# A GCN and Mamba stack on one core: stage A takes its tiles from last to first, multiplies adj by known x1 columns there, and the rest is one stream over the scans

## The reference, cut to what matters

```python
def gnn(x1, x2):                              # L = 3, W: 128 x 128
    ax1, ax2 = 2 * (adj @ x1), 2 * (adj @ x2)      # eps is 0: ax + (1 + eps) * ax
    for i in range(3):
        ax1 = relu(ax1 @ W1[i].T + b1[i]); ax2 = relu(ax2 @ W2[i].T + b2[i])
    return concatenate((ax1, ax2), 1) @ Wm.T + bm
x1 = layernorm(x + gnn(x, x2))
h = layernorm(relu(adj @ x1 @ gcn_w + gcn_b)) * ln_g + ln_b
xz = h @ w_in; u = silu(causal_conv4(xz[:, :256])); z = xz[:, 256:]
dt, B, C = split(u @ w_xp); dt = softplus(dt @ w_dt + b_dt)
for t in range(4096):                         # 256 channels x 16 states
    state = exp(dt[t] * A) * state + dt[t] * B[t] * u[t]
    y[t] = state @ C[t]
out = layernorm(x1 + ((y + u * D) * silu(z)) @ w_out)
```

## Time and profile before

| | us |
|---|---|
| median of 3 runs (1179.34 to 1181.56) | 1180.63 |
| profiled execution | 1176.16 |
| its span | 1174.6 |
| TensorE busy (with overlapping records) | 1017.3 |
| VectorE busy | 1058.9 |
| ScalarE (ACT) busy | 515.5 |
| GpSimd busy | 325.1 |

### The profile page before, as it was taken

One profiled execution on the slowest core, in us unless ns is written; L12 is line 12 of the kernel. 1 busy time (PEld: TensorE's weight loads), 2 busy tenths in 40 slices (PEclk: granted clock), 3 DMA queues, 4 the chain that ended last, 5 costly groups with the idle time before them and its releaser, 6 DMA issues. The chain is left out here.

```text
span 1174.6 us, 13465 instructions
## 1 busy us (share of the span) xinstructions
PE 1017.3 (87%) x4242; PEld 703.8 (60%) x4242; DVE 1058.9 (90%) x864; ACT 515.5 (44%) x914; POOL 325.1 (28%) x208
## 2 busy tenths in 40 slices
PE   2789999989999999999988989989889798785665
PEld 1567776767777777444555646656556455553454
DVE  5899999999999998713999999999989999999995
ACT  3344333333334242224555555736456456455431
POOL 5100101000000101001245273463632734537330
PEclk9899999999999999999998999989999899795666
DMA  9999999999999999847444253254442532101000
GB/s 259 247 189 326 318 317 330 317 335 303 348 302 350 308 335 271 174 160 257 148 150 165 91 193 139 84 190 149 145 155 80 196 143 73 36 20 53 20 26 9
DMA packets 190907, 226.43 MB, mean 193 GB/s; under 512 B 8608, under 2 KB 164320, under 8 KB 176528
## 3 DMA queue, kind: packets, MB, share of 16 engines
q1 hardware_dynamic: 107008, 165.69, 44.3%
q10 hardware_dynamic: 80768, 52.70, 18.3%
q0 software_dynamic: 3088, 7.54, 2.3%
HBM read 162.72 MB, written 63.18 MB: 192 GB/s over the span
## 5 line engine op out<-in xcount | busy, mean ns | idle before, releaser
L774 DVE STREAM_TRANSPOSE at<-rows 128x1024 f32<-128x1024 f32 x136 | 267.0, 2003 | 27.1 <-DMA rows<-in_adj 14.9
L979 PE MATMUL yT<-ah,xh 128*128 128x512 f32 x512 | 214.1, 418 | 54.5 <-DVE al L782 54.5
L486 POOL TENSOR_TENSOR dBuP<-dtu,b_sb 128x1024 f32<-128x1024 f32 x64 | 166.0, 2594 | 271.0 <-DVE hs L915 208.0
L527 ACT ACTIVATE ah<-at 128x2048 fp32r<-128x2048 f32 x64 | 122.5, 1913 | 241.0 <-PE yT L979 229.9
L1066 PE MATMUL bank<-adjc,xm 128*128 128x512 f32 x448 | 216.8, 614 | 0.8 <-ACT axT L591 0.8
L979 PE MATMUL yT<-al,xh 128*128 128x512 f32 x512 | 201.4, 393 | 0.0
L979 PE MATMUL yT<-ah,xl 128*128 128x512 f32 x512 | 201.3, 393 | 0.0
L1148 PE MATMUL yT<-ident,pr 128*128 128x128 f32 x1024 | 160.8, 312 | 24.0 <-DVE pr L922 24.0
L915 DVE TENSOR_TENSOR_SCAN hs<-dA,zero,dBuP 128x1026 f32<-128x1026 f32 x64 | 166.9, 2609 | 8.3 <-ACT dA L681 8.3
L681 ACT ACTIVATE dA<-dt,A_sb 128x512 f32<-128x512 f32 x256 | 169.4, 712 | 9.2 <-POOL dt L467 6.4
L1148 PEld LDWEIGHTS yT<-ident,pr 128*128 128x128 f32 x1024 | 142.3, 163 | 49.7 <-DVE pr L922 33.8
(11 more groups left out here) (148 smaller groups left out, 1049.0 us busy)
## 6 DMA issues: line engine op xcount, KB each, us to landing
adjT<-at SPq DMA_DIRECT2D x56, 1024.0 KB, 7.8
adjc<-adjT SPq DMA_DIRECT2D x56, 1024.0 KB, 4.9
rows<-in_adj SPq DMA_DIRECT2D x152, 256.0 KB, 8.9
rows<-in_adj ACTq DMA_DIRECT2D x136, 256.0 KB, 9.1
b_sb<-b_dram ACTq DMA_DIRECT2D x32, 512.0 KB, 3.8
xm<-in_x SPq DMA_DIRECT2D x4, 512.0 KB, 15.7
xs<-in_L_gnn_x SPq DMA_DIRECT2D x4, 512.0 KB, 14.9
res<-in_x POOLq DMA_DIRECT2D x8, 256.0 KB, 7.6
```

The source lines that it names most:

```text
L486: nc.gpsimd.tensor_tensor(dBu(n, par)[:, :, 1:], dtu[par][:, :, :], b_sb[pair % 2][:, nB(n) % 2:nB(n) % 2 + 1, :].to_broadcast([P, H, TILE ...
L527: nc.scalar.activation(ah[c % 2][:, :], at[c % 2][:, :, :].rearrange("p m t -> p (m t)"), ACT.Copy)\
L774: last = nc.vector.transpose(dst.rearrange("p m (g i) -> p g m i", i=32), src.rearrange("p g (i m) -> p g m i", i=32))
L979: last = mm(acc[k][:, :], w[:, b, :], v[c % 2][:, cols], start=(b == 0 and j == 0), stop=(b == KB - 1 and j == 2))
```

## The change

1. Stage A goes through the tiles from 7 to 0 (`t` is the step, `i = 7 - t` the tile, `s` the place of a chunk in its step). Tile j's x1 is normed in step 8-j and split into fp32r parts `x1h`, `x1l` a step later (`split_x1`). Columns with known x1, `c >= i + 2`, get the third product in stage A: 12 matmuls more in `extra`, which add into `accB`; 21 chunks in all. The partial sums of tiles 1 to 5 go through DRAM (`part_dram`), tile 0's stays in `accB`. These chunks aren't stored.
2. Tile 7's chunks are needed again, since x1 isn't known at first: they are read and transposed a second time and stored, two in each of the steps 4 to 7 (`AGAIN`), at `s` = 2 and 5. 41 chunks are stored, where it was 56.
3. After stage A, tile 0 lacks 8 blocks (chunks 1 and 0, still in `at`), four of them behind the last norm; tile 1 has 12 blocks; the other tiles have 152, where they had 192. `BLOCKS` lists them, `STEPS` and `stream()` share them out over windows 0 to 5 as one sequence, and `front_ax` follows as each sum is done.
4. The norm writes x1 straight into `xm`. The order of its rows is that of a reordering in the third layer's ACT write (and of y's copy later), so `mid`, its loads, and the residual's loads go. ACT issues the output's stores.
5. For tile 0, z is made ahead of the convolution, in banks of its own. The gcn of tile 1 stands ahead of window 0.
6. The tap transposes move into step 1. `adjc` now lies where `rows` was, so its first loads wait for the last transposes of stage A. All loops are written out.

```diff
+ORDER = [tuple(range(CHUNKS))] * (TILES - 1) + [(3, 4, 5, 6, 7, 2, 0, 1)]
+FIRST = TILES - 1
+AGAIN = {(t, s): 2 * (t - 4) + k for t in range(4, TILES) for k, s in enumerate((2, 5))}
+def known(i):
+    return range(i + 2, CHUNKS)
+def sequence():
+    seq = []
+    for t in range(TILES):
+        for s in range(CHUNKS):
+            i, c = TILES - 1 - t, ORDER[t][s]
+            seq.append((i, c, CHUNKS * t + s, t > 0 and i > 0 and c not in known(i)))
+            if (t, s) in AGAIN:
+                seq.append((FIRST, AGAIN[t, s], None, True))
+    return seq
...
+BLOCKS = [(a, j, m) for a in range(1, TILES) for j in ((1, 2, 0) if a == 1 else range(min(a + 2, CHUNKS))) for m in range(CH)]
...
+            def transpose(n):
+                dve.wait_ge(rows_in[n % NROWS], 16 * Q * (n // NROWS + 1))
+                if n >= 2:
+                    k = SEQ[n - 2][2]
+                    if k is not None:
+                        dve.wait_ge(chunk_low, k + 1)
+                    if SEQ[n - 2][3]:
+                        dve.wait_ge(chunk_stored[n % 2], 16 * stored_before(n))
...
+            def stage_a(t):
+                for s in range(CHUNKS):
+                    k = CHUNKS * t + s
+                    transpose(AT_N[k])
...
+                    if k > 0 and (t, s - 1) not in AGAIN:
+                        lo(k - 1)
...
+                    if t > 1 and s == 2:
+                        split_x1(t - 2)
+                    if t > 0 and s == 6:
+                        norm_stats(t - 1)
+                    if t > 0 and s == 7:
+                        norm_apply(t - 1)
+                    if (t, s) in AGAIN:
+                        transpose(AT_N[k] + 1)
+                        lo(k)
...
+            def extra(t, s):
+                i, c = TILES - 1 - t, ORDER[t][s]
+                pe.wait_ge(x1_low, TILES - c)
+                if c == EXTRA_FIRST[t] and t > 2:
+                    pe.wait_ge(part_copied, t - 2)
+                for m in range(CH):
+                    b = CH * (c - JX) + m
+                    cols = slice(m * TILE, (m + 1) * TILE)
+                    for j, (w, v) in enumerate(((x1h, ah), (x1l, ah), (x1h, al))):
+                        last = mm(accB[:, :], w[:, b, :], v[s % 2][:, cols], start=(c == EXTRA_FIRST[t] and m == 0 and j == 0),
+                                  stop=(i > 0 and c == CHUNKS - 1 and m == CH - 1 and j == 2))
+                return last
...
             for l in range(LAYERS):
                 layer(TILES - 1, l)
+                tile0(1, l, l + 1)
             merge(TILES - 1)
+            tile0(1, LAYERS, CH)
+            tile0(0, 0, CH)
...
             front_gcn(0)
+            adj_blocks(range(0, 7))
             front_tr(0)
+            adj_blocks(range(7, 8))
+            front_z(0, 0)
+            front_z(0, 1)
             front_xc(0, 0, TAPS)
             front_xc(0, TAPS, H * TAPS)
             front_dbc(0, 0)
+            adj_blocks(range(8, 9))
             front_dtp(0, 0)
             pe.wait_ge(selectors_ready, 4)
             spread_B(0, 0, 0)
+            adj_blocks(range(9, 12))
+            front_gcn(1)
+            for b in range(TILES):
+                window(b, b % 2, b > 0, b < TILES - 1)
```

More of the change, by code:

```diff
@@ L110, in gnn_mamba @@
         A = ExitStack()
+        NROWS = 4
+        rows = [sb(f"rows{k}", [P, GROUPS, P], F32, A) for k in range(NROWS)]
         xh = [sb(f"xh{k}", [P, KB, D], F32R, A) for k in range(2)]
@@ L299, in load_x @@
                         .then_inc(x_in[2 * part + k], 16)
-            load_rows(sp, (0, 1), 0, 0)
+            load_rows(sp, (0, 1), 0)
             load_x(0)
             for c in range(1, NROWS):
-                load_rows(sp, (0, 1), 0, c)
+                load_rows(sp, (0, 1), c)
                 load_x(c)
[L307 to L314, removed]
@@ L330, in load_adj @@
[L330 to L336, removed]
@@ L338, in load_res @@
[L338 to L353, removed]
@@ L356, in _ @@
[L356 to L364, removed]
+            for n, (i, c, k, st) in enumerate(SEQ):
+                sp.wait_ge(chunk_turned, n + 1)
+                if st:
+                    sp.dma_start(adjT[((i - 1) * CHUNKS + c) * P:((i - 1) * CHUNKS + c + 1) * P, :],
+                                 at[n % 2][:, :, :].rearrange("p m t -> p (m t)")).then_inc(chunk_stored[n % 2], 16)
+                if n + NROWS < len(SEQ):
+                    load_rows(sp, (0, 1), n + NROWS)
@@ new lines, in _, with adj_blocks @@
+            tile0(0, 0, CH)
+            def adj_blocks(ks):
+                for k in ks:
+                    a, j, m = BLOCKS[k]
+                    q = k // CH
+                    begins = k == 0 or BLOCKS[k - 1][0] != a
+                    ends = k + 1 == len(BLOCKS) or BLOCKS[k + 1][0] != a
+                    if begins:
+                        pe.wait_ge(ax1_ready, a)
+                        if a in PARTS:
+                            pe.wait_ge(part_loaded, 16 * a)
+                            mm(accB[:, :], ident[:, :], part_in[:, :], start=True, stop=False).then_inc(part_used, 1)
+                    if m == 0:
+                        pe.wait_ge(adjT_in[q % NADJ], 16 * (q // NADJ + 1))
+                    last = mm(accB[:, :], xm[:, CH * j + m, :], adjc[q % NADJ][:, m, :], start=(begins and a not in PARTS), stop=ends)
+                    if ends:
```

517 lines of the change are left out of this document (262 added, 255 removed).

## The result

The changed kernel takes 1211.2 us, median of four runs (1206.3 to 1212.5), against 1180.9 beside it: ratio 1.0251, 95% interval 1.0220 to 1.0281. It is slower, as forecast, but by twice as much: 30.3 us where 14.7 were forecast, and 1195.3 us with a range up to 1206. The profiled executions differ by more, 1212.5 against 1176.2 us, spans 1210.7 against 1174.6, because the one of before lay under its median and this one over it.

What follows compares the result with a forecast made beforehand. VectorE bounds stage A and the scan windows, TensorE the handover between. Terms: stage A +49.3, handover -18.3, first window -10.9, windows -5.4, together +14.7 us on the median 1180.6, giving 1195.3 us, range 1177 to 1206 (own course 1188 to 1201).

Steps and rivals of the forecast that it cites:

- The change's sign and its reason: Whole kernel: slower, chance 0.80; blocks taken out of VectorE-bound windows give nothing, anything put into stage A costs time.
- Stage A, TensorE: Stage A: up to step 5 TensorE's 61.6 us a tile fits VectorE's 63.1; then TensorE sets the end, +49.3 us.
- The begin of the heavy stretch: Stage A, `lo` of step 6, place 3: done at 405.3 against 377.6, with store waits +6 and -2.3 us.
- TensorE's last stretch: Stage A from step 6, place 3: eleven heavy chunks, two plain ones and the MLP take 110 us, ending at 515.3.
- rival A: End of stage A: VectorE, not TensorE, ends it; end -9.6 us, 1185.7 us; chance 0.15.
- rival C: Stage A: stores of chunks read again land late, 3.3 us for each of five, +10.5, 1205.8 us; chance 0.11.
- rival B: Stage A: fewer stores relieve traffic, VectorE's chunk 6.0 not 6.30 us, sum -2.5, 1178.1 us; chance 0.14 for it or more.
- Handover: Last product of stage A to first scan: 60.1 us instead of 78.4, -18.3 us.
- the term for the clock: Handover: half clock behind TensorE's uncovered 4.5 us wait costs 2.5 us, bounds 0 and 3.4 (two stretches).
- rival D: Handover: not shortened as far, another chain takes 3 to 5 us of the 18, 1199 us; chance 0.08.
- First window: Scan 0 to scan 1: gcn of tile 1 stands before window 0, scan 1 at 550.3 rather than 561.2, -10.9 us.
- Windows: Scan windows: 40 blocks leaving give nothing; unrolled loops -3.1, small waits for spread banks 2.3 less; -5.4 us.

Runs made afterwards that it cites:

- experiment 4: Changed kernel with early x1 products for tiles 0 and 1 only, blocks of tiles 2 to 5 back in the windows: 1193.7 us, ratio 1.0118.
- experiment 1: Changed kernel with one matmul (x1h ah) instead of three in the early product: 1188.6 us, ratio 1.0076.
- experiment 3: Changed kernel with second readings moved: to places 1 and 3 of steps 4 to 7, 1217.3 us; all eight in steps 6 and 7, 1202.0 us.
- experiment 5: Changed kernel with chunks of three stacks placed between chunks of two in steps 4 to 6: 1207.6 us, ratio 1.0241.
- experiment 2: Changed kernel without second readings, tile 7's chunks stored in step 0: 1204.7 us, ratio 1.0213.
- experiment 6: Changed kernel with nine unread filler products in TensorE's two longest handover waits: 1208.3 us; also with ACT's relu moved later in window 0: 1209.3 us.
- experiment 7: Kernel before the change with the loops over windows 2 to 5 written out on all engines: 1178.9 us, ratio 0.9999.
- experiment 8: Changed kernel, early products for tiles 0 and 1 only, fillers; eight chunks stored in step 0: 1181.1 us; last, two stored, six reread in steps 6, 7: 1175.0.

## Why the prediction was right in direction and wrong in size

**The change's sign and its reason** stood: blocks moved out of windows that VectorE bounds bring nothing and cost in stage A (experiment 4: the edit for 10 chunks, 15.6 us, for nothing), and the handover and the first window give back less than stage A takes.

**The step that failed** is the one in "Stage A, TensorE": "Up to `t` = 5 a tile ... still fits into VectorE's 54.3 + 0.85 + 7.9 = 63.1." The 63.1 us hold only for steps 4 and 5, which have two readings each. Step 3 has none: VectorE's sum is 54.3 + 0.85 = 55.2 us, and TensorE's by the same prices (216 matmuls and the layers) 56.1, so it didn't fit even as a sum. The step took 55.9 us (norms at 172.80 and 228.67), and TensorE didn't wait between 189 and 237 us. For steps 4 and 5 the comparison is right as a sum, and both engines have room in it, but they don't have it at the same time. `ah` and `al` have two buffers, so neither can be more than two chunks ahead. Behind a second reading TensorE has nothing to do (4.35 us at 304.17), and during its 8.15 us chunks VectorE waits for `ah`. Measured: 14.9 us of waiting ahead of step 6, place 3, gone to 0.3 without the ten chunks (experiment 4), and to 3.8 in all with lighter ones (experiment 1). I had put 0 for it. The begin of the heavy stretch came 8.9 us later than predicted; the sum had 3.7 us for stores, and the store waits there are 5.3 us, where the kernel before had 4.5 up to the same chunk, so that term was too high by 2.9 and hid part of the miss. The waits view of before also has 4.2 us of short waits of its transposes for `lo`, which the changed kernel's doesn't have: 14.9 - 2.9 - 4.2 leaves 7.8 of the 8.9. How the waits come about is settled in part. Most of them, 12.2 of 14.9 us, stand at the second chunk of a step, where ACT's `ah` comes behind the end of TensorE's last heavy chunk and behind the copy of the partial sum (324.10). The place of the second readings (experiment 3) isn't it, the clustering (experiment 5) at most a third. The copies, the half clock behind TensorE's waits (1.6 us at 304) and a third `ah` buffer weren't tried apart.

**TensorE's last stretch** was sized right: 110 us, measured 111.3, and 109.8 in experiment 4. So rival A (VectorE ends the stage) was wrong. The row's 0.2265 us a matmul held in the changed kernel. The 215.7 ns of TensorE: Matmul & The Clock Gate, of the Trainium skill ("Wait — 56ns, not 53.3ns?"), would have given 4.8 us less for the stretch and isn't seen.

**Stores** (rival C) were not the reason: 1.2 us a reading predicted, 0.26 to 1.65 shown. They can be: 11.9 us with the readings at places 1 and 3.

**Traffic relief** (rival B) didn't come: a `lo` or transpose takes what it took, and the store waits are 5.3 us where they were 4.5. Storing eight more in step 0 does cost: the first norm came 11.9 us later in experiment 2.

**Handover.** All operations ran as listed; the term for the clock was mis-sized. I took 2.5 us for one to two stretches at half clock of 3.4 us, as the trace of before showed one. It was some 14 us, in two stretches of 7. That is at most 7 us lost, an estimate that takes TensorE for the chain's pace all through. Filling the two waits gave 4.5 us and the predicted 3.7 us for the eight matmuls (experiment 6), with 7 us near half clock left. The 2.4 us behind ACT's relu I hadn't seen at all: of the moved gcn of tile 1 I costed TensorE's side, and not what ACT's relu has queued behind it. In all 5.2 us of the 18.3 were missing, near what rival D had said (3 to 5).

**First window**: -11.4 for -10.9, right.

**Windows**: -0.9 for -5.4. The back edge is real (77.2 for 79.4 in experiment 7), but its time isn't gained, not even in the kernel before. Window 1 gave 1.5 us back in waits for spread banks; experiment 6 shows the same, larger. That the bank comes late because TensorE, with less to do, runs at half clock there (0.91 granted in window 1, where the kernel before had 0.94 in its own) was only argued. The 2.0 us of the tail lie in the output product, for which VectorE waits 7.77 us in the changed kernel and 4.87 in the one before, at 0.60 and 0.80 granted (1189 to 1206 and 1155 to 1170 us). The moved blocks aren't needed for that: the kernel before with its loops written out waits 8.03 us there, at 0.57 (1156 to 1173).

## What to carry to other kernels

Two engines that pass chunks through two buffers aren't bounded by the sum of a step alone: before work is put into an engine's slack, look where the slack lies, whether the buffers let it be used, and what a third engine between the two has to do first. Compare the sums for each step by itself, too: a step without the added work has less room. Take work out of a stage only where its engine is that stage's bound; here 10 of 21 moved chunks came from windows in which TensorE waited anyway. And work that a change adds (here the second readings) costs less behind the point from which the other engine is the bound, though not nothing (five readings: 18.4 us won in front, 10.6 lost behind): that, dropping the ten chunks, and the fillers made it 36 us cheaper.

## What the runs showed of the hardware that I had not expected

A wait of 4.51 us in TensorE was followed by two stretches of some 7 us at half clock, 0.62 and 0.61 granted over the 15 us, though TensorE was busy 6.89 of the first 8 and all of the next 7; the same wait filled with products that nobody reads brought the next eight matmuls from 6.55 to 3.70 us. Eight 1 MB stores in the first step, beside the first loads, put the first norm 11.9 us back (130.72 for 118.82, experiment 2). That isn't a price for each: in the last kernel of experiment 8, with two of them, the norm comes at 119.52, where experiment 4 without any has 119.23.
